# Fused attention and mixture-of-experts kernel: chosen rows divided ahead of local rows, rows of maxima sent from ScalarE's queue

## The reference

```python
x = x + layernorm(attention(layernorm(x), Wq, bq, Wk, bk, Wv, bv))
x = x + layernorm(moe(layernorm(x), Wg, W1, W3, W2, sw1, sw3, sw2))

# attention: 16 heads of 32; every block of 128 queries sees the 256 keys around it (64 on either side)
scores = einsum('nhbqd,nhbkd->nhbqk', qb, kb) / sqrt(d)
scores = where(valid, scores, -1e9)
ctx = einsum('nhbqk,nhbkd->nhbqd', softmax(scores), vb).reshape(n, h, t, d)
# 64 chosen queries of each head (first, last, the 62 of largest norm) see all 1024 keys
qg = take_along_axis(q, idx[..., None], axis=-2)
g_ctx = einsum('nhqk,nhkd->nhqd', softmax(einsum('nhqd,nhkd->nhqk', qg, k) / sqrt(d)), v)
ctx = ctx.at[bn, bh, idx].set(g_ctx)
```

## Time and profile before

| | |
|---|---|
| median of 3 runs | 823.47 us (823.22 to 826.71) |
| the profiled execution | 823.6 us |
| its span | 821.8 us |
| mean granted clock of TensorE | 0.989 |
| TensorE busy | 777.9 us (95% of the span) |
| VectorE, ScalarE, GpSimd busy | 563.3, 422.9, 146.1 us |
| DMA queues | q1 (issued by SyncE) 153.54 MB, q0 (issued by GpSimd) 7.97 MB |

### The profile page before, as it was taken

The page is one execution under the profiler, slowest core; times in us unless marked ns, Lnnn a source line. Parts: engine busy times, 40 slices in busy tenths (PEclk is TensorE's granted clock), DMA queues, the critical chain, the costliest instruction groups (busy, mean ns, idle before and its releaser), DMA issues.

```text
span 821.8 us, 13879 instructions
## 1 busy us (share of the span) xinstructions
PE 777.9 (95%) x5060; PEld 651.3 (79%) x5060; DVE 563.3 (69%) x1196; ACT 422.9 (51%) x839; POOL 146.1 (18%) x229
## 2 busy tenths in 40 slices
PE   6999999999999999898999999999999999999994
PEld 4787887777777777676877887999999999887883
DVE  5764897578987566676588545466776666758666
ACT  5464352455656566666544244566675666723120
POOL 3300010410112014232344432000000000013122
PEclk9999999999999999999999999999999999999998
DMA  7789465975676788772339622676787776546444
GB/s 234 228 277 347 164 204 174 268 221 164 173 218 167 195 216 223 210 197 93 104 133 322 238 95 90 193 214 209 220 241 227 236 232 212 170 149 200 152 154 141
DMA packets 117492, 162.39 MB, mean 198 GB/s; under 512 B 17364, under 2 KB 65236, under 8 KB 117424
## 3 DMA queue, kind: packets, MB, share of 16 engines
q1 hardware_dynamic: 113840, 153.54, 61.8%
q0 software_dynamic: 3584, 7.97, 3.2%
HBM read 107.24 MB, written 55.05 MB: 197 GB/s over the span
## 4 chain that ended last, share of the span: by engine, by line
PE 65%; DVE 18%; DMA 5%; ACT 4%; issue 3%; POOL 1%; SPq 0%; POOLq 0%; DVEq 0%; ACTq 0%
PE bank L163 43%; PE wide L163 17%; DVE MX L160 4%; PE wide L167 3%; PE bank L167 2%; DVE SG L160 2%; DMA XX<-scr_xd 2%; DVE STC L281 1%; DMA scr_q<-hl 1%; DVE GC L153 1%; DMA scr_qtok<-H2A 1%; ACT PTG L145 1%; DMA H2A<-scr_oe,FG 1%; ACT PT L157 1%; DVE SIL L149 1%
## 5 line engine op out<-in xcount | busy, mean ns | idle before, releaser
L163 PE MATMUL wide<-W2H,HH 128*128 128x512 f32 x308 | 101.8, 396 | 0.5 <-ACT OUTR L145 0.5
L160 DVE TENSOR_REDUCE MX<-wide 128x1 f32<-128x192 f32 (+1 forms) x128 | 77.6, 647 | 20.9 <-PE wide L163 20.9
L157 ACT ACTIVATE PT<-bank 128x512 f32<-128x512 f32 x128 | 73.4, 593 | 29.1 <-PE bank L163 29.0
L157 ACT ACTIVATE SIL<-bank 128x256 f32<-128x256 f32 (+1 forms) x72 | 32.7, 454 | 98.1 <-PE bank L163 97.8
L149 DVE TENSOR_TENSOR SIL<-bank,SIL 128x256 f32<-128x256 f32 (+1 forms) x72 | 36.9, 512 | 64.0 <-ACT SIL L157 63.3
L163 PE MATMUL bank<-XT,W13H 128*128 128x256 f32 (+1 forms) x336 | 76.6, 322 | 0.0
L145 ACT ACTIVATE HH<-SIL 128x256 fp32r<-128x256 f32 (+1 forms) x72 | 35.2, 489 | 66.6 <-DVE SIL L149 66.6
L163 PEld LDWEIGHTS wide<-W2H,HH 128*128 128x128 f32 x308 | 58.6, 190 | 13.3 <-ACT OUTR L145 1.3
L149 DVE TENSOR_TENSOR HH<-SIL,HH 128x256 fp32r<-128x256 f32 (+1 forms) x72 | 37.0, 514 | 45.9 <-ACT HH L145 37.7
L163 PE MATMUL wide<-W2L,HH 128*128 128x512 f32 x168 | 66.5, 396 | 0.8 <-DVE W2L L149 0.7
L163 PEld LDWEIGHTS bank<-XT,W13H 128*128 128x128 f32 x336 | 55.0, 188 | 4.7
(11 more groups left out here) (256 smaller groups left out, 2010.4 us busy)
## 6 DMA issues: line engine op xcount, KB each, us to landing
R<-in_L_ffn_W_dram SPq DMA_DIRECT2D x48, 512.0 KB, 5.6
scr_q<-hl SPq DMA_DIRECT2D x16, 512.0 KB, 4.3
scr_k<-hl SPq DMA_DIRECT2D x16, 512.0 KB, 4.1
R<-in_L_ffn_sw_dram SPq DMA_DIRECT2D x12, 512.0 KB, 5.4
QSe<-scr_q SPq DMA_DIRECT2D x36, 128.0 KB, 3.7
KSe<-scr_k SPq DMA_DIRECT2D x36, 128.0 KB, 3.7
R<-_attn_hidden_states_dram SPq DMA_DIRECT2D x16, 256.0 KB, 3.9
scr_qtok<-H2A SPq DMA_DIRECT2D x16, 256.0 KB, 3.8
```

Source lines behind the costliest of these rows:

```text
L157: return do("act", lambda g: g.activation(dst, src, fn, **kw), after)
L160: return do("dve", lambda g: g.tensor_reduce(dst, src, AXX, op), after)
L163: return do("pe", lambda g: g.matmul(ps, a, b, start=start, stop=stop, skip_group_check=True), after, mark=mark)
```

## The change

`row_shift` issues its DMA from ScalarE, right behind the copy that fills its source. `global_back` takes no bank of `ST_`; it writes 64 columns of the second half of the `W_` buffer in which `global_values` accumulated its result. That buffer is released by the last division in `global_finish` and not by the copy to `OS`. In slot 1 `global_back` and `global_finish` come ahead of `local_turn` and `local_finish`. And `h_mean2`, `h_h2` and `h_turn` of the tiles 0 to 3 each come one slot later.

```diff
@@ row_shift
-            hd["m_row"] = dma("sp", row_slots[hd["qi"]], lambda g: g.dma_start(
+            hd["m_row"] = dma("act", row_slots[hd["qi"]], lambda g: g.dma_start(
                 f(qb[96:97, :]).rearrange("o (b q) -> o b q", q=P), f(rw[:, :])), [m_c])
@@ global_values
                 m_c = copy("act", os[:, 0:P], w[:, 0:P], [m_o] + sfree)
-                W_.busy[g_["wi"]].append(m_c)
                 g_["os"] = (si, os, m_c)
+                g_["back"] = (g_["wi"], w[:, 512:576])
@@ global_back
                 si, os, m_c = g_["os"]
-                ti, tb, tfree = ST_.take()
-                g_["back"] = (ti, tb)
-                g_["m_t"] = mm(tb[:, 0:64], os[:, 0:P], twice[:, :], True, True, [m_c, m_two] + tfree, mark=True)
+                g_["m_t"] = mm(g_["back"][1], os[:, 0:P], twice[:, :], True, True, [m_c, m_two], mark=True)
@@ global_finish
-                ti, tb = g_["back"]
+                wi, tb = g_["back"]
...
-                ST_.busy[ti].append(m_f)
+                W_.busy[wi].append(m_f)
@@ slot_of
-            H_AT = {0: h_mean, 5: h_x1, 7: h_mean2, 8: h_h2, 10: h_turn}
+            H_AT = {0: h_mean, 5: h_x1, 8: h_mean2, 9: h_h2, 11: h_turn}
...
+                if k == 1 and i > 0:
+                    global_back(i - 1)
+                    global_finish(i - 1)
                 if g >= 5 and g % 4 == 1:
                     local_turn((g - 5) // 4)
                     local_finish((g - 5) // 4)
-                if k == 1 and i > 0:
-                    global_back(i - 1)
-                    global_finish(i - 1)
                 if k == 1 and i < 16:
                     global_max(i)
```

## The result

The changed kernel takes 861.74 us (median of 4 runs, 855.93 to 863.27) against 825.03 us of the kernel before in the same comparison: a ratio of 1.0423 with a 95% interval of 1.0384 to 1.0461. I had forecast 822.2 us in a range of 815.5 to 829 us. It is clearly slower, and far outside. (The ratio is estimated from all runs together and differs a little from the quotient of the two medians, 1.0445.)

A forecast was written before the change was run, and what follows sets the result against it. TensorE was taken to bound the kernel, busy 47.2 of 50 us from 200 us on. From 823.6 us, 0 + 1.0 + 1.6 - 0.3 - 0.7 - 3.0 = -1.4 gave 822.2 us, range 815.5 to 829.

The forecast's parts named there:

- Part 1: Slot 1, product with `twice` in `W_` ahead of the local turn: a round gains 0.3 us, bounds 0 to 0.5.
- the late row: Row of maxima issued at 331.51 us; TensorE waited until 336.30 and its clock fell, a cost of 3.0 us.
- the 15 x 0.3 of the sum: The 0.3 us a round gained from the order of slot 1, taken over 15 rounds.
- Part 2: Row's DMA on ScalarE: 0.68 us an issue, PTG of slot 4 0.5 us later, net +0.2 us a round with Part 1.
- where I had put nothing: Rounds 0 to 5: the net +0.2 us is hidden behind slot 0's wait for the maxima, 6 x 0 = 0.
- I count the event as gone: -3.0 us: On ScalarE's queue the row needn't stand behind SyncE's loads and its window grows, so the late row goes: -3.0 us.
- the late row stays or another takes its place: Rival: the loads crowd elsewhere and the 3.0 us aren't saved, +1.6 us on the whole, 825.2 us; chance 0.12.
- The dear issue: Rival: SyncE and ScalarE take turns at issuing, a slot-4 row takes 1.2 us, +7 us on the sum, 829 us; chance 0.15.
- Part 3: Rounds 11 to 14, later token-tile steps: PTG 0.4 to 0.5 us later, +1.6 us; once -0.7 us in round 11.
- +1.6 us: Rounds 11 to 14: the tile turn's ScalarE copy, now behind PG, delays PTG; four rounds at +0.4 us.
- The 0.7 us of round 11: VectorE's maxima come ahead of the late statistics, so TensorE's 0.67 us wait for its `W_` buffer goes: -0.7 us, once.

The follow-up runs named there:

- e2: Kernel before with only the product with `twice` in the `W_` buffer and ahead of the local turn: 820.29 us, ratio 1.0002 to the kernel before.
- e10: The kernel of e2 run again: 820.59 us against 823.65 of the kernel before, ratio 0.9967.
- e9: Changed kernel with a bare wait for MR left in SyncE's list and `h_h2` ahead of slot 1's VectorE work: 823.44 us, 0.9987 of the kernel before.
- e7: Changed kernel with the rows back on SyncE's queue and `h_h2` ahead of `global_back` in slot 1: 821.81 us, ratio 0.9951 to the kernel before.
- e1: Kernel before with one edit, the rows of maxima issued by ScalarE: 841.61 us, ratio 1.0239 to the kernel before.
- e3: Kernel before with only `h_mean2`, `h_h2` and `h_turn` of tiles 0 to 3 one slot later: 834.94 us, ratio 1.0145 to the kernel before.
- e4: Changed kernel with the rows of maxima back on SyncE's queue: 830.98 us, ratio 1.0102 to the kernel before.

## Why the prediction was wrong

**Part 1, the order of slot 1: right in the round, and not all of it in the medians.** The rounds of 13.28 us in e2 stand against 13.57 and 13.58 us in the rounds from 275 us on before (from one copy MR of slot 4 to the next), the 0.3 us that I worked out; the rounds between 190 and 260 us take 13.86 to 13.89 us against 14.17 to 14.20. The last copy MR starts at 382.1 us before, at 375.3 in e2 and at 375.2 in e10. Of these 6.8 us 3.0 are the late row, which only the profile before has; 3.8 are left, near the 15 x 0.3 of the sum. The lists of waits don't show it, since the waits for MX grew by nearly as much as those for GC fell. The medians of e2 and e10 show only 0 to 3 us. The rest of the program took 2.4 us more in e10's profile than before (442.1 against 439.7 us) with no edit there, so a gain of this size drowns in what varies anyway; whether that is the whole reason stays open.

**Part 2, the issue: the size was right, the sentence behind it wrong.** ScalarE's issues take 0.63 us, PTG of slot 4 starts 0.7 us behind the end of MR, and TensorE waits up to 0.3 us for PTG in slot 6. With the loads held back, the price of a round can be read: in the rounds from 275 us on, e9 takes 13.74 to 13.75 us, e7 with the old queue 13.27 to 13.28, and before 13.57 and 13.58. The issue costs 0.5 us there and, net of part 1, 0.2 us, both as forecast. In the rounds between 190 and 260 us, where I had put nothing, e9 takes 13.9 us as e7 does, against 14.2 before: the issue is hidden, and the gain of part 1 isn't. The step that failed reads: "SyncE stood 45.7 us behind MR in 19 waits; now its loads run ahead until a buffer is not free. No wait of TensorE names a load, so this gives nothing; it does crowd the loads to other moments." The waits for MR were what spread SyncE's loads over the round, and left the queue with little in it when a row was sent. I looked for a transfer that would come late with the loads and named only the loads; the late one is the row itself, whose window of 2.8 us I had worked out in the paragraph before. With it fell "I count the event as gone: -3.0 us": one event became eight, 12.2 us of standing plus the clock. I had the case as the rival "the late row stays or another takes its place", at +3 us and a chance of 0.12: its mechanism was right and its size far off (e1 is 20 us slower for this edit alone), since I priced one event and not eight of up to 3.4 us.

Of the two sections of the Trainium skill's page "DMA: Bandwidth & Descriptors" that I set against each other, the runs bear out "Issuing engines are not separate DMA queues": the row shares the 16 engines with the loads, and took 5.5 to 6.8 us in a queue that carried nothing but such rows. A ring of its own ("Queues, rings and completion order") did not protect it. No run tells which packets it stood behind.

**The dear issue**, my rival on the slow side, did not come: the median issue was 0.63 us, and only one took 1.23. Taking turns at issuing was no cost here.

**Part 3, the later steps: the wrong place in a queue.** This is the second step that failed. I worked out what `h_turn` brings to ScalarE behind PG (+1.6 us) and have no term for `h_h2`: its step from slot 0 to slot 1 was put at nothing without a reason. I did not ask what stands ahead of its 0.15 us product on VectorE: at the end of slot 1 that is the GC division, the local division and the maximum, 2.5 us of work, which itself waits for TensorE. e3 is 1.0145 for this edit alone, some 12 us, and e7 takes it away by moving one step. The 0.7 us of round 11 were real (no such wait is left in e3 or e7) but no match.

**The clock.** I priced a fall of the clock once, at 1.3 us, with the one late row. In the changed kernel 12 waits of up to 3.4 us came with 19.2 us of longer matmuls, as much as the standing itself. In its trace a stand of TensorE of 1.29 us and each of 2.16 us and more was followed by 20 products that took 2.8 to 3.6 us for 1.93, and 1.55 us by 3.22 before; the stands of 0.95 us and less were not. Over the whole profile the added matmul time was 10.8 us beside 8.1 us of added idle time in e1, 8.6 beside 5.6 in e3, and 3.4 beside 6.0 in e4.

## What to carry to other kernels

When an issue leaves an in-order queue, its wait leaves with it. Ask what that wait held back, and check each small transfer with a tight window against what now flies beside it; if the wait was a brake worth having, leave a bare wait in its place. When a step is moved by a slot, read the queue of every engine that it uses at its new place, above all for the small instruction on which a large one hangs. And add the clock to the price of any new stand of TensorE of more than a microsecond: here it took 0.6 to 1.5 times as much again.

## What the hardware showed that I had not expected

A 4 KB row on a queue with no other traffic took 5.5 to 6.8 us until it could be read, behind a backlog of loads on the other queue. On SyncE's queue in the kernel before, a row took 2.8 us or less where the loads before it had been held back, even at a momentary DMA share of 0.91. And the same row's issue on ScalarE takes 0.63 us to a single partition of on-chip memory and 0.27 us to a row in HBM.
